# Layer 0's cross attention: contraction of the 96 channels in three chunks of 32 in place of 64 + 32, with scores on 32-row tiles, weighing on 32-column tiles, and the queries issued ahead of the scores

## What is computed

```python
x = x + _L0_xattn_ref(_layernorm(x, axis=-1), ctx_768, Wq, Wk, Wv, Wo, bo)

def _L0_xattn_ref(x, context, Wq, Wk, Wv, Wo, bo):      # 16 heads of 64
    q = (x @ Wq).reshape(B, Nq, h, dh)
    k = (context @ Wk).reshape(B, Nk, h, dh)
    v = (context @ Wv).reshape(B, Nk, h, dh)
    scores = einsum('bqhd,bkhd->bhqk', q, k) / sqrt(dh)
    attn = softmax(scores, axis=-1)
    out = einsum('bhqk,bkhd->bqhd', attn, v).reshape(B, Nq, h * dh)
    return out @ Wo + bo
```

## Time and profile before

| | us |
|---|---|
| median of 3 runs (lowest, highest) | 3038.8 (3036.45, 3040.16) |
| the profiled execution's own time | 3039.36 |
| its span, first to last instruction | 3037.6 |
| the changed stage's 30 inner tiles, 87.15 to 834.00 | 746.85 |
| PE busy in these (its share) | 713.48 (96%) |

### The profile page before, as it was taken

How to read it: one execution, slowest core, us unless ns; L and a number is a source line. 1 busy time by engine, 2 the same in 40 slices (tenths; PEclk the granted TensorE clock), 3 DMA queues, 4 the chain that set the end, 5 groups by cost and what they waited for, 6 DMA issues and landing times. The chain is left out here.

```text
span 3037.6 us, 86653 instructions
## 1 busy us (share of the span) xinstructions
PE 2684.9 (88%) x34695; PEld 2075.7 (68%) x34695; DVE 1814.9 (60%) x3282; ACT 1459.1 (48%) x3915; POOL 1086.9 (36%) x1037
## 2 busy tenths in 40 slices
PE   6999999999978999998567785899999888599998
PEld 4666666666656888886445553677777676488887
DVE  2444444444466666666589987677777565644443
ACT  2444444444434666665422221777777443244443
POOL 1333333333320000003157675566666331133332
PEclk7999999999999999998689998899999796799999
DMA  4211111111100000000100000201100001000000
GB/s 127 105 57 57 57 57 57 57 57 57 58 1 1 0 0 0 0 0 1 48 0 0 0 0 4 68 26 29 29 26 26 2 0 45 1 0 0 0 0 28
DMA packets 37427, 82.19 MB, mean 27 GB/s; under 512 B 4709, under 2 KB 18665, under 8 KB 36713
## 3 DMA queue, kind: packets, MB, share of 16 engines
q1 hardware_dynamic: 37354, 81.16, 8.3%
HBM read 76.96 MB, written 4.19 MB: 27 GB/s over the span
## 5 line engine op out<-in xcount | busy, mean ns | idle before, releaser
L501 ACT ACTIVATE l_probs<-ps,l_nmax 128x257 f32<-128x257 f32 x512 | 236.2, 474 | 326.7 <-DVE l_nmax L439 326.7
L535 POOL TENSOR_TENSOR l_probs<-l_probs,l_rden 128x1024 f32<-128x1024 f32 x128 | 242.6, 1895 | 385.3 <-DVE l_rden L445 385.3
L942 POOL TENSOR_TENSOR l_probs<-l_probs,l_rden 128x1024 f32<-128x1024 f32 x128 | 242.5, 1895 | 171.9 <-DVE l_rden L812 171.9
L439 DVE TENSOR_REDUCE l_nmax<-ps 128x2 f32<-128x514 f32 x256 | 165.4, 688 | 179.9 <-PE ps L335 179.9
L2395 POOL TENSOR_TENSOR m_hh<-m_hh,m_comb_t 128x512 f32<-128x512 f32 (+1 forms) x160 | 142.9, 901 | 341.0 <-DVE m_hh L2345 341.0
L882 ACT ACTIVATE l_probs<-ps,l_nmax 128x257 f32<-128x257 f32 x512 | 236.3, 474 | 57.4 <-DVE l_nmax L806 57.3
L2345 DVE TENSOR_TENSOR m_hh<-ps,m_sg 128x512 f32<-128x512 f32 (+1 forms) x160 | 95.8, 599 | 225.3 <-ACT m_sg L2309 225.3
L806 DVE TENSOR_REDUCE l_nmax<-ps 128x2 f32<-128x514 f32 x256 | 165.4, 688 | 65.8 <-PE ps L712 62.9
L817 DVE COPY l_pT<-ps 128x512 f32<-128x512 f32 x256 | 164.9, 686 | 53.8 <-PE ps L721 49.6
L1372 POOL CAST enc_xt<-enc_xs 128x256 fp32r (+1 forms) x32 | 12.8, 402 | 463.7 <-PE ps L138 396.5
L365 PE MATMUL ps<-ident,l_probs 128*128 128x128 f32 x1024 | 139.0, 279 | 35.4 <-ACT l_xnT L495 34.5
(11 more groups left out here) (343 smaller groups left out, 7036.7 us busy)
## 6 DMA issues: line engine op xcount, KB each, us to landing
l_ctxA<-in_ctx_a SPq DMA_DIRECT2D x32, 514.0 KB, 3.8
l_ctxB<-in_ctx_b SPq DMA_DIRECT2D x32, 514.0 KB, 4.7
l_ctxT<-in_ctx_t SPq DMA_DIRECT2D x32, 385.5 KB, 3.3
l_ctxK<-in_ctx_k SPq DMA_DIRECT2D x32, 384.0 KB, 5.1
x<-in_x SPq DMA_DIRECT2D x4, 512.0 KB, 7.1
scratch<-l_W SPq DMA_DIRECT2D x2, 1024.0 KB, 6.9
l_last_w<-scratch SPq DMA_DIRECT2D x32, 64.0 KB
out_x<-x SPq DMA_DIRECT2D x1, 2048.0 KB, 8.7
```

What stands on the lines that cost most here:

```text
L439: nc.vector.tensor_reduce(nmax[:, par, 2 * half:2 * half + 2], ps[:, S_B + 2 * half:S_B + 2 * half + 2, 0:NK], AX.X, ALU.max, negate=True) ...
L501: nc.scalar.activation(probs[:, par, hg, :], ps[:, S_B + hg, 0:NK], ACT.Exp, bias=nmax[:, par, hg:hg + 1], accum_out=den[:, par, hg:hg + 1 ...
L535: nc.gpsimd.tensor_tensor(pr, pr, rden[:, b, :, None].to_broadcast([P, HG, NK - 1]), ALU.mult).then_inc(norm_ok, 1)
L942: nc.gpsimd.tensor_tensor(pr, pr, rden[:, b, :, None].to_broadcast([P, HG, K_W]), ALU.mult).then_inc(norm_ok, 1)
```

## The change

The context for the scores is laid out by the host as three chunks of 32 channels, each repeated on the four groups of 32 partitions (`ctxQ`), in place of `ctxA` (64 channels twice) and `ctxB` (32 channels four times). Scores are 12 matmuls on 32-row tiles, weighing is 24 matmuls on 32-column tiles, and `A2`, `U2` are folded in the same layout. TensorE's order in a unit becomes queries or turn_x, scores, weighing, transposes, heads. The queries go to bank 5 in place of 4. `sum_heads` runs in units b = 1..3 with 4 matmuls each, in place of b = 0..3 with 3. The copy to `xnT` moves from ScalarE to VectorE; on VectorE the query copy moves ahead of the maxima and the `pT` copy ahead of the inversion; on ScalarE the `pT` copy moves ahead of the `oT` move; each half of the transposes signals by itself. The load of `ctxQ` waits for the scores of tile t, that of `ctxK` for its weighings.

```diff
-def stage_xattn(nc, k, w, ctx_a, ctx_b, ctx_k, ctx_l, last_mask, scratch, next_loads, x_dram, ident):
+def stage_xattn(nc, k, w, ctx_q, ctx_k, ctx_l, last_mask, scratch, next_loads, x_dram, ident):
...
-                pe.wait_ge(a_sb, 8)
+                pe.wait_ge(a_sb, 4)
                 pe.nop(nofuse=True)
                 for h in range(H):
-                    c, q, i = h // 2, 64 * (h % 2), h % HG
-                    hg, half, s = h // HG, 64 * (h // 8), h // HG % 2
-                    at_s = (2 * s + i // 2) * D
-                    nc.tensor.matmul(ps[half:half + 64, i % 2, at_s:at_s + D], wvT[q:q + 64, c, 0:64],
-                                     wo[q:q + 64, c, :], start=True, stop=True)
-                    last = nc.tensor.matmul(ps[N * hg:N * hg + N, 2 + i % 2, (i // 2) * D:(i // 2) * D + D],
-                                            wvT[q:q + 64, c, 64:C], wo[q:q + 64, c, :], start=True, stop=True)
+                    c, q, i, r = h // 2, 64 * (h % 2), h % HG, N * (h // HG)
+                    for n in range(NQ):
+                        last = nc.tensor.matmul(ps[r:r + N, 2 * (i % 2) + n // 2, (2 * (n % 2) + i // 2) * D:
+                                                   (2 * (n % 2) + i // 2) * D + D],
+                                                wvT[q:q + 64, c, N * n:N * n + N], wo[q:q + 64, c, :],
+                                                start=True, stop=True)
...
-                        to_a = A2[:, g, par:HG:2, :].rearrange("p c (r m) -> p c r m", r=2)
-                        nc.scalar.mul(to_a, made_a[:, :, :, 0:64], scale).then_inc(a_sb, 1)
-                        to_b = A2[:, 2, par:HG:2, 64 * g:64 * g + 64].rearrange("p c (r m) -> p c r m", r=2)
-                        nc.scalar.mul(to_b, made_a[:, :, :, 64:C], scale).then_inc(a_sb, 1)
+                        for n in range(NQ):
+                            to = A2[:, n, par:HG:2, 2 * N * g:2 * N * g + 2 * N].rearrange("p c (r m) -> p c r m", r=2)
+                            last = nc.scalar.mul(to, made_a[:, :, :, N * n:N * n + N], scale)
+                        last.then_inc(a_sb, 1)
...
-            def load(t, j):
-                for dst, src in ((ctxA[:, j, :], ctx_a), (ctxB[:, j, :], ctx_b), (ctxK[:, j, :], ctx_k)):
-                    sp.dma_start(dst, src[bass.ds(t, 1), :, :].rearrange("t c n -> c (t n)")).then_inc(ctx_in[j], 16)
-
-            load(0, 0)
+            def load_q(t, j):
+                sp.dma_start(ctxQ[:, j, :, :].rearrange("p c n -> p (c n)"), ctx_q[bass.ds(t, 1), :, :].rearrange(
+                    "t c n -> c (t n)")).then_inc(ctx_in[j], 16)
+
+            def load_k(t, j):
+                sp.dma_start(ctxK[:, j, :], ctx_k[bass.ds(t, 1), :, :].rearrange(
+                    "t c n -> c (t n)")).then_inc(ctx_in[j], 16)
+
+            load_q(0, 0)
+            load_k(0, 0)
...
             with sp.Fori(1, T // 2) as i:
                 for j in range(2):
+                    sp.wait_ge(s_mm, 4 * (2 * i + j) - 4)
+                    load_q(2 * i + j, j)
                     sp.wait_ge(o_mm, 4 * (2 * i + j) - 4)
-                    load(2 * i + j, j)
+                    load_k(2 * i + j, j)
...
-            def queries(i):
+            def queries(c):
 
                 for h in range(HG):
-                    last_i = nc.tensor.matmul(ps[:, T_B, h * P:h * P + P], A2[:, i, h, :], xnT[:, :],
+                    last_i = nc.tensor.matmul(ps[:, T_B + 1, h * P:h * P + P], A2[:, c, h, :], xnT[:, :],
                                               start=True, stop=True)
                 last_i.then_inc(q_mm, 1)
 
-            def scores(b, j, after):
-
-                keys = slice(b * NK, b * NK + NK)
-                for hg in range(HG):
-                    if after is not None and hg % 2 == 0:
-                        pe.wait_ge(exp_ok, 4 * after + hg + 2)
-                    r = 64 * (hg % 2)
-                    nc.tensor.matmul(ps[:, S_B + hg, 0:NK], q1[r:r + 64, j, hg // 2, b, :], ctxA[r:r + 64, j, keys],
-                                     start=True, stop=False)
-                for hg in range(HG):
-                    r = N * hg
-                    last_i = nc.tensor.matmul(ps[:, S_B + hg, 0:NK], q1[r:r + N, j, 2, b, :], ctxB[r:r + N, j, keys],
-                                              start=False, stop=True)
-                    if hg % 2:
-                        last_i.then_inc(s_mm, 1)
-
-            def sum_heads(b, j, t):
-
-                if b == 0:
+            def scores(b, j):
+
+                for c in range(NQ):
+                    for hg in range(HG):
+                        r = N * hg
+                        last_i = nc.tensor.matmul(ps[:, S_B + hg, 0:NK], q1[r:r + N, j, c, b, :],
+                                                  ctxQ[r:r + N, j, c, b * NK:b * NK + NK], start=c == 0, stop=c == NQ - 1)
+                last_i.then_inc(s_mm, 1)
+
+            def sum_heads(n, j, t):
+
+                if n == 0:
                     pe.wait_ge(o_sb, 4 * t + 5)
                     pe.wait_ge(x_ok, t + 1)
-                for i in range(NQ * b, NQ * b + NQ):
+                for i in range(HG * n, HG * n + HG):
                     nc.tensor.matmul(ps[:, A_B, 0:D], oT[:, j, i, :, :].rearrange("c b n -> c (b n)"), U2[:, i, :],
                                      start=i == 0, stop=False)
-                if b == SEQ - 1:
...
-                last_i.then_inc(t_mm, 1)
+                    last_i.then_inc(t_mm, 1)
...
-                for kt in range(2):
-                    at_k = (b * 2 + kt) * C
-                    for r in range(2):
-                        nc.tensor.matmul(ps[64 * r:64 * r + 64, O_B, 0:2 * P], ctxK[:, j, at_k:at_k + 64],
-                                         pT[:, kt, 2 * P * r:2 * P * r + 2 * P], start=kt == 0, stop=kt == 1)
-                for kt in range(2):
-                    at_k = (b * 2 + kt) * C + 64
-                    for hg in range(HG):
-                        last_i = nc.tensor.matmul(ps[N * hg:N * hg + N, O_B, 2 * P:3 * P], ctxK[:, j, at_k:at_k + N],
-                                                  pT[:, kt, P * hg:P * hg + P], start=kt == 0, stop=kt == 1)
+                for c in range(NQ):
+                    for kt in range(2):
+                        at_k = (b * 2 + kt) * C + N * c
+                        for hg in range(HG):
+                            last_i = nc.tensor.matmul(ps[N * hg:N * hg + N, O_B, c * P:c * P + P],
+                                                      ctxK[:, j, at_k:at_k + N], pT[:, kt, P * hg:P * hg + P],
+                                                      start=kt == 0, stop=kt == 1)
...
-                    if b < SEQ - 1:
-                        scores(b + 1, j, u)
-                    elif not last:
-                        pe.wait_ge(q_sb, NQ * t + 2 * NQ)
-                        pe.wait_ge(ctx_in[1 - j], 48 * fills)
-                        scores(0, 1 - j, u)
                     if has_query:
-                        if start_unit:
-                            pe.wait_ge(xt_sb, 2)
-                        else:
-                            pe.wait_ge(pt_a, u)
+                        if b == 0:
+                            pe.wait_ge(xt_sb, t + 2)
+                        if not start_unit:
+                            pe.wait_ge(pt_v, u)
                         queries(b)
                     if has_x:
                         pe.wait_ge(pt_v, u)
                         turn_x(t + 2)
+                    if b < SEQ - 1:
+                        pe.wait_ge(exp_ok, 4 * u + 4)
+                        scores(b + 1, j)
+                    elif not last:
+                        pe.wait_ge(q_sb, NQ * t + 2 * NQ)
+                        pe.wait_ge(ctx_in[1 - j], 32 * fills)
+                        pe.wait_ge(exp_ok, 4 * u + 4)
+                        scores(0, 1 - j)
                     if not start_unit:
                         weigh_ctx(u - 1, (b - 1) % SEQ, j if b else 1 - j)
                     turn_probs(t, b, has_query, has_x)
-                    if not first:
-                        sum_heads(b, 1 - j, t - 1)
+                    if b and not first:
+                        sum_heads(b - 1, 1 - j, t - 1)
...
+            pe.wait_ge(q_sb, NQ)
             turn_x(1)
-            pe.wait_ge(q_sb, NQ)
-            pe.wait_ge(ctx_in[0], 48)
-            scores(0, 0, None)
+            pe.wait_ge(ctx_in[0], 32)
+            scores(0, 0)
...
-                                      ps[:, T_B, :].rearrange("c (h b n) -> c h b n", h=HG, b=SEQ)).then_inc(q_sb, 1)
+                                      ps[:, T_B + 1, :].rearrange("c (h b n) -> c h b n", h=HG, b=SEQ)
+                                      ).then_inc(q_sb, 1)
+
+            def turned(t):
+                dve.wait_ge(xt_mm, t + 1)
+                nc.vector.tensor_copy(xnT[:, :], ps[:, T_B + 1, 0:P]).then_inc(xt_sb, 1)
 
             def maxima(u, par):
+                dve.wait_ge(s_mm, u + 1)
```

(60 more changed lines are left out.)

14 lines of the change are left out of this document (6 added, 8 removed).

## The result

The changed kernel takes 2967.8 (2964.6 to 2973.5, four runs) against 3039.5 for the kernel before in the runs beside it: ratio 0.974, 95% interval [0.971, 0.978]. It is faster by 71.7; the forecast was 2975, with a range from 2957 to 3000. The profiled execution's span is 2962.7, 74.9 shorter than before.

The account below looks back on a forecast made before the run. TensorE was taken as the bound, busy for 88% of the span. Savings of 59.4 + 0.7 + 2 + 1.5 = 63.6 from the profiled 3039.4 gave 2975.8, which stood 0.6 above the median, so 2975; range 2957 to 3000.

Parts of the forecast that it names:

- Rounds stay the same, changes of tiling go: Inner-tile units: array rounds unchanged, fewer tiling changes; scores 1.50 in place of 1.71, weighing 1.43 in place of 1.59.
- rival 3: Scores to weighing: joining row and column tiles costs twice today's 0.22, 26 over the stage, 3001; chance 6%.
- A wait goes: Unit b = 3: the transposes' 1.15 wait for ScalarE's copy to xnT disappears.
- A wait comes: Queries wait for VectorE's pT copy: 0.97 ahead of b = 1, 0.07 behind b = 1 and b = 2.
- Rival 2: VectorE's pT copy late each time: large delay 3038, no change, chance 4%; small delay 2985 to 3000, 10%.
- Issue as a bound: Weighing: if passes kept 40 ns, each weighing costs 0.62 more, 74 over the stage, 3049; chance 4%.
- The other engines' slack: Exponentials, inversion and GpSimd in the loop finish in time; exponentials have slack of 0.8 at least, costing nothing.
- the folding: Folding U2 at the start: 96 passes take 16 in place of 16.7, 0.7 less; kept -6 to +4.
- the 30 tiles: Inner tiles of the stage: 22.92 in place of 24.90 each, 1.98 a tile, 59.4 together.
- the opening: Start of the loop: queries run inside the scores' wait for exponentials, 2 less.
- the end: Last tile, without queries: only changes of tiling saved, less one short wait for exponentials, 1.5 less.
- rival 4: Tiling changes save less or queries start as early as L365; with full-clock folding and short joins 2958; chance 10%.

Follow-up runs that it names:

- e1: The kernel before with only the new 32-channel chunks in folding, loads, scores and weighing; order, banks and waits of before: 0.981 of the kernel before (2988.7).
- e2: The changed kernel with the old 64 + 32 tiling and folding put back, new order, banks and waits kept: 0.995 of the kernel before (3031.8).
- e8: The kernel before with ScalarE's xnT copy moved ahead of the exponentials of unit b = 3: 0.988 of the kernel before (3006.8).
- e4: The changed kernel with the transposes of bank 5 issued before those of bank 4: 0.969 of the kernel before (2952.0).
- e7: The changed kernel with bank 5's transposes first and a tile's head sums in four threes: 0.965 of the kernel before (2934.9).
- e6: The changed kernel with the folding's eight even heads issued first, then the eight odd ones: 0.975 of the kernel before.
- e3: The kernel before with its 64-column and 32-column folding matmuls in two separate loops: 0.995 of the kernel before (3031.3).

## Why the prediction was right, and where it was not

**Rounds stay the same, changes of tiling go: right.** Scores were summed at 1.50 and cost 1.51, weighing at 1.43 and 1.45, and the units, b = 0 to 3, came out at 5.82, 5.93, 6.00 and 5.26, where the sum had 5.83, 5.92, 5.92 and 5.25. The tile is 23.01 for 22.92. The join of row and column tiles, taken over from L335 ahead of L377 in the last tile, costs what it did there, so rival 3 did not come. e1 shows the mechanism alone: 0.17 a change in a loop where nothing else moved. e2 shows the change of tiling that the new order saves, which the sum had inside its terms for queries and head sums.

**A wait goes: right, and a little larger than its row.** e8 gives 1.19 a tile for the 1.15 that the row showed.

**A wait comes: right in b = 1** (0.94 for 0.97); the short ones behind b = 1 and b = 2 were put at 0.07 each and cost 0.06 and 0.14 at the gap, besides 0.09 and 0.05 in the groups behind them, whose first weights were not loaded ahead (e4). It is the copy alone that sets them: e4 takes 0.43 from the first by letting the copy start 4 transposes sooner, and e7 covers the rest. Rival 2 (the copy late each time) did not come.

**Issue as a bound: did not come.** 48 passes of weighing take 1.45 from start to start, 30 ns each, which is near the 27 that their array rounds ask, and no row of PE in a steady unit has a wait but that for the copy. By the 62 ns that the Trainium skill (TensorE: Matmul & The Clock Gate, "Wait — 56ns, not 53.3ns?") gives for a MATMUL with hardware decode off, the weighing would have taken 2.98, as an estimate. The trace has 1.45, so that bound was not in force here, as the row of 128 passes in 1.25 had said; whether hardware decode was on stands in no row.

**The other engines' slack held:** PE has no wait for exponentials, `norm_ok` or `oT` in the steady tiles.

**The step that failed in size is the folding**, the term "I take 16, 0.7 less, and keep -6 to +4". The program's first scores start 15.3 earlier, outside what I had kept; 12.5 earlier, as against e2 and e8, is outside too. Two things were missed. First, I priced the 96 new passes as if each had to wait for the one before (0.107 or twice that). They took 5.13, because passes on the two row halves run beside each other (e6), and 16.7 - 5.13 = 11.5 was saved where I had 0.7. Second, I carried the half clock of that stretch over as given (up to 20), while the alternation of the old folding had brought it about (e3). Without the alternation it stays at full level, and the wide matmuls L217, which I had not touched at all, gain 3.4 (2.7 against e2 and e8).

**How near the number is owes something to luck.** The other terms were summed at 62.9, and without the folding the stage came out 58.6 shorter: 56.0 for 59.4 in the 30 tiles (a tile after is 0.09 more than summed, and one before 24.87 on average, not 24.90), 1.5 for 2 at the opening, 1.1 for 1.5 at the end. The folding gave 14.6 more than summed and the rest 4.3 less. The two errors went opposite ways, and so 2967.8 stands 7 below 2975. Of rival 4, half came (the folding at the full clock), and half did not (cheaper changes of tiling, queries that start as L365 does).

## What to carry to other kernels

Count the changes of TensorE's tiling as one counts instructions: with fixed array work, four 32-row tiles and four 32-column tiles in two unbroken runs beat 64 + 32 although they take 72 passes in place of 40. Groups of two passes on one tile between changes were the worst case: each change cost no more than in the loop, but no two tiles ever worked at once, and the clock fell. Before an edit that reorders for one wait, look for the engine queue that makes the copy late: two lines on ScalarE gave half of this change. And before a reordering is praised for a wait that went, subtract the wait that came: here they cancel, and what the order gave is a change of tiling. When a group is put ahead of the copy that frees its bank, issue first the work that the copy needs, and put other matmuls behind it; the granted clock of a stretch is a result of what is issued there, not a given.

## What the runs showed of the hardware that was not expected

A change of tiling cost 0.17 in the loop, between groups of 8 to 48 passes, and 0.13 in the folding of before, between groups of two (0.345 for a group at the full clock, 17.73 to 18.09 to 18.43, less two passes of 0.109).

The granted clock fell from its full level of 2.4 GHz to 1.2 GHz with PE busy in the records all the time. What TensorE had done before was that alternation, for 3 in before and for 6.2 in e2 and e8. It fell there in every kernel that has the alternation and in none without it (changed, e1, e3, e4, e6, e7), though e6's folding alone lasts 7.8.

Passes of 128 columns on one tile start 0.109 apart; how many ns a pass costs on average is set by how many tiles are at work. In e3, 32 passes on eight tiles of 64 rows by 32 columns took 0.70, 22 ns each: they start in four rounds of eight. The changed kernel's order has two tiles at work on the same tile shape (54 ns), e6's one or two (81 ns). With tiles taken from the order of the code, the first pass on the next tile started when four passes of the tile before were left, the one just started among them: with the 9th of 12 in e6, the 3rd of 6 in the changed kernel, the 5th of 8 in L210 of e3, and with the first of 4 in L214 of e3. No run varied this by itself.
